# One product for B and C, dt out of the scores, two-bank VectorE instructions, and a third of the decay weighing on GpSimd

## What is computed

```
proj = rmsnorm(modulated layernorm(x)) @ in_proj_w.T      # z 256, x_ssm 256, B 128, C 128, dt 4
xh   = silu(causal conv of x_ssm, 4 taps);  dt = softplus(dt_raw + dt_bias);  dA = exp(-exp(A_log) * dt)
h_t  = h_{t-1} * dA_t + (dt_t * xh_t) B_t;  y_t = h_t . C_t + D * xh_t     # 4 heads of 64
x1   = x + ga * (h_in + (y * silu(z)) @ out_proj_w.T)
logits = rmsnorm(modulated layernorm(x1)) . slots;  dispatch = softmax over tokens, combine = softmax over slots
out  = x1 + gb * combine( experts( dispatch(x) ) )
```

## Time and profile before

| | us |
|---|---|
| median of 3 runs (230.20 to 232.47) | 231.29 |
| span of the profiled execution | 227.2 |
| busy: PE / PEld | 205.5 (90%) / 148.2 (65%) |
| busy: DVE / ACT / POOL | 139.5 (61%) / 120.3 (53%) / 60.9 (27%) |
| chain that ended last, by engine | PE 68%, DVE 11%, ACT 11%, POOL 4%, DMA 3% |
| granted TensorE clock | 1.00 (2.4 GHz) throughout |

### The profile page before, as it was taken

One profiled execution on the slowest core, in us unless ns is written; L12 is line 12 of the kernel. 1 busy time (PEld: TensorE's weight loads), 2 busy tenths in 40 slices (PEclk: granted clock), 3 DMA queues, 4 the chain that ended last, 5 costly groups with the idle time before them and its releaser, 6 DMA issues.

```text
span 227.2 us, 4247 instructions
## 1 busy us (share of the span) xinstructions
PE 205.5 (90%) x1575; PEld 148.2 (65%) x1575; DVE 139.5 (61%) x372; ACT 120.3 (53%) x264; POOL 60.9 (27%) x147
## 2 busy tenths in 40 slices
PE   3879979995799899998978799989999999999995
PEld 2445555673377795475656387765865948659995
DVE  3887868998999956859988875730130221302753
ACT  3879896533468856797531566658327062270000
POOL 6545885016524203984015600000000000000000
PEclk9999999999999999999999999999999999999999
DMA  6404000200600000000500000006222141200122
GB/s 189 118 6 140 1 5 8 87 3 11 197 24 3 0 0 3 1 2 7 183 0 1 0 3 0 0 3 185 49 84 61 42 139 49 85 10 3 46 69 69
DMA packets 15344, 10.72 MB, mean 47 GB/s; under 512 B 1773, under 2 KB 13654, under 8 KB 15326
## 3 DMA queue, kind: packets, MB, share of 16 engines
q1 hardware_dynamic: 15100, 10.31, 15.5%
q10 hardware_dynamic: 226, 0.16, 0.2%
HBM read 9.34 MB, written 1.07 MB: 46 GB/s over the span
## 4 chain that ended last, share of the span: by engine, by line
PE 68%; DVE 11%; ACT 11%; POOL 4%; DMA 3%; issue 2%; ACTq 1%; DVEq 0%; POOLq 0%
PE bank L577 28%; PE bank L922 13%; PE bank L904 11%; PE bank L761 4%; PE bank L814 3%; PE bank L750 2%; POOL root L490 2%; DVE xcT L1309 2%; DVE bst L1183 2%; ACT zsT L1066 2%; PE bank L829 2%; DMA vec_nat<-ffn_slot_norm_gamma_dram 2%; ACT xhT L1072 1%; PE bank L835 1%; PE bank L860 1%
## 5 line engine op out<-in xcount | busy, mean ns | idle before, releaser
L1446 DVE TENSOR_TENSOR eo<-bank,seg_e 128x512 f32<-128x512 f32 x8 | 5.5, 692 | 47.9 <-PE bank L922 47.9
L922 PEld LDWEIGHTS bank<-w_sb,zsT 128*64 128x64 f32 x256 | 27.8, 137 | 3.0 <-issue 3.0
L922 PE MATMUL bank<-w_sb,xcT 128*64 128x128 f32 x256 | 28.8, 273 | 0.0
L922 PE MATMUL bank<-w_sb,zsT 128*64 128x128 f32 x256 | 28.8, 273 | 0.0
L922 PEld LDWEIGHTS bank<-w_sb,xcT 128*64 128x64 f32 x256 | 27.8, 137 | 0.0
L904 PE MATMUL bank<-slotsT,w_sb 128*128 128x512 f32 (+1 forms) x64 | 26.1, 558 | 0.2 <-ACT zsT L1140 0.2
L1140 ACT ACTIVATE zsT<-bank,vecT 128x512 f32<-128x512 f32 x16 | 10.7, 687 | 24.9 <-PE bank L904 24.9
L577 PE MATMUL bank<-xnT,winT 128*128 128x512 f32 x48 | 23.0, 607 | 0.3 <-ACT BT L1053 0.3
L490 POOL TENSOR_TENSOR root<-root,neg_half 128x2 f32<-128x2 f32 (+1 forms) x24 | 20.2, 842 | 2.0
L904 PEld LDWEIGHTS bank<-slotsT,w_sb 128*128 128x128 f32 x64 | 11.4, 190 | 12.6 <-issue 12.1
L1309 DVE SCALAR_TENSOR_TENSOR xcT<-bank,convw,xcT 128x510 f32<-128x510 f32 (+2 forms) x24 | 17.3, 737 | 3.6 <-ACT xcT L1050 3.3
(11 more groups left out here) (165 smaller groups left out, 414.9 us busy)
## 6 DMA issues: line engine op xcount, KB each, us to landing
w_sb<-in_L_ffn_w_dram SPq DMA_DIRECT2D x16, 256.0 KB, 2.9
mods_bc<-mod_dram SPq DMA_DIRECT2D x4, 320.0 KB, 3.5
xin<-in_L_attn_x_dram SPq DMA_DIRECT2D x4, 256.0 KB, 3.1
out_dram<-x1tok SPq DMA_DIRECT2D x16, 64.0 KB, 1.5
mods_bc<-mod_dram SPq DMA_DIRECT2D x4, 192.0 KB, 3.3
seg_e<-mod_dram SPq DMA_DIRECT2D x1, 512.0 KB, 3.8
eo<-in_L_attn_in_proj_w_dram SPq DMA_DIRECT2D x1, 384.0 KB, 4.1
eo<-in_L_wmod_dram SPq DMA_DIRECT2D x1, 256.0 KB, 4.6
```

What stands on the lines that cost most here:

```text
L922: q = nc.tensor.matmul(o[j * S:(j + 1) * S, tile_cols(b)], act_h[j][k // 2][:, k % 2, at:at + S], w2_sb[j][:, k, :], start=k == 0 and b == ...
L1446: V.tensor_tensor(o, bank[4 + 2 * (it % 2) + g][:, :].rearrange("p (b d) -> p b d", d=P), b2_bc[:, it, :].unsqueeze(1).broadcast_to((P, 4, ...
```

## The change

1. B and C are no longer projected. Once, at the start, TensorE multiplies the two 128x128 blocks of the weights; with that product U = (M xn) of one projection, and G = xn_s . U_t, so `scores` takes xnT itself as one operand. U is copied by `copy_u` (with the norm's weight as scale).
2. The four dt columns are appended to U (`dt_columns`, GpSimd, once), so dt_raw comes out of the score matmuls: 260 and 132 columns in place of 256 and 128. `dt_in` reads `gm`, after `copy_scores`. Scores now go to banks 4j+3 and 4j+2, before z, and no longer wait for the convolution.
3. PSUM is one tensor `banks`; `dt_times_x`, `token_max`, `slot_max` and `norm_slots` run once over both halves in place of twice.
4. `weigh(2)` and `weigh(5)` become `weigh_last(0)` and `weigh_last(1)` on GpSimd; `decay(5)` and `y_of` wait for them.
5. All tables of turns are new, SP's too; `rsm_rows(1)` goes from turn 13 to 30, `slots` and `xn2T` have tiles of their own, `mod_rows` shares `combT`.

```diff
 
+            def dt_columns():
+
+                pool.wait_ge(s_act0, ACT_WIN)
+                for j in range(2):
+                    nc.gpsimd.tensor_copy(ut[j][:, :, L:L + H], winT[:, U0 + P:U0 + GB].unsqueeze(1).broadcast_to((P, BP, H))
+                                          ).then_inc(s_ut, 1)
...
+            def weigh_last(bi):
+                def visit(j, it):
+                    wait(pool, g_done, j, it, bi + 1)
+                    wait(pool, seg_done, j, it, 3 * bi + 3)
+                    if bi:
+                        wait(pool, y_ps, j, it, 1)
+                    else:
+                        wait_before(pool, disp_done, j, it)
+                    s = gm[j][:, bi * GW + L + H:(bi + 1) * GW - H]
+                    nc.gpsimd.tensor_tensor(seg_m[j][:, 2, :].rearrange("p (h t) -> p h t", h=H),
+                                            seg_e[j][:, 2, :].rearrange("p (h t) -> p h t", h=H),
+                                            s.unsqueeze(1).broadcast_to((P, H, P)), ALU.mult
+                                            ).then_inc(m_last_done[1][j], 1)
+                return visit
...
                 wait(pe, xnT_done, j, it)
                 if it == 0:
                     pe.wait_ge(s_act0, (ACT_WIN, ACT_SN)[j])
-                for t in range(TP):
-                    q = mm(b3[:, t * H:(t + 1) * H], xnT[j][:, tile_cols(t)], winT[:, DT0:ROWS])
-                q.then_inc(proj_ps[1][j], 1)
+                wait_before(pe, slotsT_done, j, it)
+                mm(b2[:, :], winT[:, U0:U0 + P], xnT[j][:, :]).then_inc(proj_ps[1][j], 1)
 
                 wait_before(pe, slots_done, j, it)
                 mm(b0[:, :], winT[:, X0:X0 + P], xnT[j][:, :]).then_inc(proj_ps[1][j], 1)
                 mm(b1[:, :], winT[:, X0 + P:X0 + 2 * P], xnT[j][:, :]).then_inc(proj_ps[1][j], 1)
-                wait_before(pe, slotsT_done, j, it)
-                mm(b2[:, :], winT[:, B0:B0 + P], xnT[j][:, :]).then_inc(proj_ps[1][j], 1)
+
+            def scores(j, it):
+
+                wait(pe, ut_done, j, it)
+                if it == 0:
+                    pe.wait_ge(s_ut, j + 1)
+                for bi in range(BP):
+                    o = bank[4 * j + 3 - bi]
+                    mm(o[:, 0:L + H], xnT[j][:, tile_cols(bi * NT)], ut[j][:, bi, :])
+                    mm(o[:, L + H:GW], xnT[j][:, tile_cols(bi * NT + 1)], ut[j][:, bi, P:L + H]).then_inc(g_ps[1][j], 1)
 
             def project2(j, it):
 
-                wait(pe, nabs_done, j, it)
-                mm(bank[4 * j + 3][:, :], winT[:, C0:C0 + P], xnT[j][:, :]).then_inc(proj_ps[1][j], 1)
-                wait(pe, xbc_done, j, it, 3)
-                mm(bank[4 * j + 2][:, :], winT[:, Z0:Z0 + P], xnT[j][:, :]).then_inc(z_ps[1][j], 1)
+                wait(pe, g_done, j, it, 1)
+                mm(bank[4 * j + 3][:, :], winT[:, Z0:Z0 + P], xnT[j][:, :]).then_inc(z_ps[1][j], 1)
 
             def project3(j, it):
-                wait(pe, xbc_done, j, it, 4)
-                mm(bank[4 * j + 3][:, :], winT[:, Z0 + P:Z0 + 2 * P], xnT[j][:, :]).then_inc(z_ps[1][j], 1)
-
-            def scores(j, it):
-
-                wait(pe, xbc_done, j, it)
-                for bi in range(BP):
-                    wait(pe, conv_done, j, it, bi + 1)
-                    o = bank[4 * j + bi]
-                    t0 = bi * L
-                    mm(o[:, 0:L], BT[j][:, t0:t0 + P], CTr[j][:, t0:t0 + L])
-                    mm(o[:, L:L + P], BT[j][:, t0 + P:t0 + L], CTr[j][:, t0 + P:t0 + L]).then_inc(g_ps[1][j], 1)
+                wait(pe, g_done, j, it, 2)
+                mm(bank[4 * j + 2][:, :], winT[:, Z0 + P:Z0 + 2 * P], xnT[j][:, :]).then_inc(z_ps[1][j], 1)
...
-                    wait(pe, m_done, j, it, 3 * bi + 3)
+                    wait(pe, m_done, j, it, 2 * bi + 2)
+                    wait(pe, m_last_done, j, it, bi + 1)
...
-            visits = [((2, 7, 61, 64), t_xn), ((4, 9, 65, 68), project1), ((6, 11, 66, 70), project2),
...
+            visits = [((2, 7, 61, 64), t_xn), ((3, 10, 65, 68), project1), ((8, 13, 72, 70), project2),
...
+
+            def copy_u(j, it):
+                wait(act, proj_ps, j, it, 1)
+                A(ut[j][:, :, 0:L], bank[4 * j + 2][:, :].rearrange("p (b t) -> p b t", b=BP), ACT.Identity,
+                  scale=vecT[:, RNW:RNW + 1]).then_inc(ut_done[1][j], 1)
...
             def dt_in(j, it):
-                wait(dve, proj_ps, j, it, 1)
+                if it == 0:
+                    dve.wait_ge(s_small, N_SMALL)
                 d = dv[j]
-                step(j, it, V.tensor_tensor(d[:, VV, :].rearrange("p (t h) -> p t h", h=H),
-                                            bank[4 * j + 3][:, 0:TP * H].rearrange("p (t h) -> p t h", h=H),
-                                            dtb_row[:, :].unsqueeze(1).broadcast_to((P, TP, H)), ALU.add))
+                wait(dve, g_done, j, it)
+                step(j, it, V.tensor_tensor(d[:, VV, :].rearrange("p (b n h) -> p b n h", b=BP, n=NT),
+                                            gm[j][:, 0:BP * GW].rearrange("p (b c) -> p b c", b=BP)[:, :, P:GW]
+                                            .rearrange("p b (n c) -> p b n c", c=GB)[:, :, :, P:GB],
+                                            dtb_row[:, :].unsqueeze(1).unsqueeze(1).broadcast_to((P, BP, NT, H)), ALU.add))
...
             def dt_times_x(j, it):
-                for bi in range(BP):
-                    wait(dve, xht_ps, j, it, bi + 1)
-                    V.tensor_tensor(
-                        dtx[j][:, bi * NT:(bi + 1) * NT, :].rearrange("p t (h d) -> p (t h) d", h=H),
-                        bank[4 * j + bi][:, :].rearrange("p (g d) -> p g d", d=HD),
-                        dv[j][:, DTH, bi * NT * H:(bi + 1) * NT * H].unsqueeze(2).broadcast_to((P, NT * H, HD)),
-                        ALU.mult).then_inc(dtx_done[1][j], 1)
+                wait(dve, xht_ps, j, it)
+                V.tensor_tensor(
+                    dtx[j][:, :, :].rearrange("p t (h d) -> p (t h) d", h=H),
+                    banks[:, 4 * j:4 * j + 2, :].rearrange("p b (g d) -> p (b g) d", d=HD),
+                    dv[j][:, DTH, :].unsqueeze(2).broadcast_to((P, TP * H, HD)), ALU.mult).then_inc(dtx_done[1][j], 1)
...
             def slot_max(bi):
                 def visit(j, it):
-                    for m2 in range(2):
-                        wait(dve, ls_ps, j, it, 2 * bi + m2 + 1)
-                        with nc.allow_low_precision("the shift of a softmax"):
-                            q = V.reduce_max(cshift[j][:, 2 * m2:2 * m2 + 2],
-                                             bank[4 * j + (0, 2)[bi] + m2][:, :].rearrange("p (m t) -> p m t", m=2), AX.X)
-                    q.then_inc(cshift_done[1][j], 1)
+                    n0 = 4 * j + (0, 2)[bi]
+                    wait(dve, ls_ps, j, it, 2 * bi + 2)
+                    with nc.allow_low_precision("the shift of a softmax"):
+                        V.reduce_max(cshift[j][:, :].rearrange("p (n m) -> p n m", n=2),
+                                     banks[:, n0:n0 + 2, :].rearrange("p n (m t) -> p n m t", m=2), AX.X
+                                     ).then_inc(cshift_done[1][j], 1)
                 return visit
```

201 lines of the change are left out of this document (99 added, 102 removed).

## The result

| | before | after |
|---|---|---|
| median, us (4 runs each) | 231.38 (230.20 to 232.47) | 235.35 (233.80 to 236.19) |
| ratio after / before, 95% interval | | 1.016 (1.010 to 1.022) |
| span of the profiled execution | 227.2 | 231.7 |
| busy PE / PEld | 205.5 / 148.2 | 204.1 / 146.6 |
| busy DVE / ACT / POOL | 139.5 / 120.3 / 60.9 | 134.6 / 121.9 / 72.3 |

What follows compares the result with a forecast made beforehand. No single engine was taken as bound around the scans, but a relay among four; 2.1 + 1.3 from the rounds, 0.4 from softmax, 0.5 back, net 3.3, gave span 223.9 and time 228.0 us, range 224.2 to 231.2.

Steps and rivals of the forecast that it cites:

- a gain of 3.3 us: Whole kernel: 2.1 from round 0, 1.3 from round 1, 0.4 from softmax stages, 0.5 back for collisions; net 3.3 us.
- rival (1): TensorE was the bound all along, so its 7.6 us come off whole, giving 223.7 us; chance 0.16.
- Walk of round 0: Scan of round 0: first exp at 33.1 to 33.3, last output projection at 52.9 instead of 55.00; minus 2.1 us.
- Walk of round 1: Scan of round 1: first y products at 107.8 behind GpSimd's queue, last output projection 122.5 instead of 123.81; minus 1.3 us.
- 1.3 and 0.9 a pass: VectorE: 1.3 us a pass from weighings that leave, near 0.9 us a pass from two-bank forms and small reciprocals.
- The merged forms: Two-bank VectorE operations: waits for the second half, 0.4 to 0.6 us each, priced at nothing; 0.4 us gained in softmax stages.
- the list of what would prove me wrong: Signs: first exp at 34.6 or later, GpSimd weighings near 1.9 or VectorE's near 1.2, TensorE waiting for merged reductions.
- The two extra table loads: ScalarE, round 0, in the queue to ksm: two more loads of 1283 ns, 2.6 us; 5.3 by the skill's drain rule.
- Rival (2): Round 0 gives nothing: loads, late dt and rsm1 eat its gains, only round 1's 1.3 us remain; 230.0 us, chance 0.25.
- Rival (3): GpSimd's queue decides each y, its operations held 0.45 us each beside VectorE; 234.3 us at worst, chance 0.13.
- The 4.1 us stay: Whole kernel: the median 231.29 lies 4.1 us over the profiled span 227.2; this was added to the forecast span 223.9.

Runs made afterwards that it cites:

- the filled kernel: The changed kernel plus 15 matmuls that nothing reads, ahead of TensorE's waits (8 in round 0, 7 in round 1): 233.45 us, ratio 1.0047 to the kernel before.
- the control without products: The kernel before with GpSimd's basis and gate products cut to 4 of 128 columns: 231.47 against 231.62 us, ratio 0.9988.

## Why the prediction was wrong

By the ratios, the loss of 3.7 us is 2.6 of clock (1.0 to 4.2) and 1.5 of GpSimd's products (0.3 to 2.7); by the medians 235.35, 233.45 and 231.10 it would be 1.9 and 2.4. With both gone the changed kernel stands 0.4 us under the kernel before (from 1.2 under to 0.4 over), and level with it when that has the same cut (0.9983 and 0.9988). So two things went wrong: two costs that I left out, and a gain of 3.3 us that is not there even without them.

*The clock: the step that failed.* "Half of the removed matmuls stand where TensorE would then wait" was used against rival (1) only. I took TensorE idle time as free, because the trace of before has its clock at 1.00 throughout. That was one execution: in 29 later runs of the kernel before the mean clock was between 0.978 and 1.000, mostly 0.993; in the control without products (0.993) the clock was at 0.50 for 3.4 us behind the scan of round 0, from 56.7. No term of the sum allowed for it. What the runs showed in its place: 13.6 us at 0.50 in two stretches and a mean of 0.971, 2.6 us of the result.

*Walk of round 0: the other step that failed.* Three of the four table loads are where I put them (20.46, 25.55, 27.07), and ksm came at 29.43 as forecast. The fourth, at 31.8 in the walk (33.1 less 1.28), started at 33.34. I had VectorE's convolution of pass 1 from 27.0 to 31.5, "just in time" for the last silus; it ran from 28.14 to 32.66. The cast of 1.02 us and the operation of 0.63 beside GpSimd are 1.3 us more than twice 0.17, and moving the basis group away brought the load, w and the first exp forward by that much. So of the 2.1 to 2.3 us by which the first exp missed its mark (35.36 for 33.1 to 33.3), 1.5 are the load.

The rest, 0.7 us, is TensorE. I went from ksm to the first decay block without the second running sums, which stand between them in its queue and wait for w of pass 1 at 33.38, where it was 30.80 before. At full clock this costs the first exp nothing: in the filled kernel the sums wait for w just so (33.72), and the exp follows its load without a gap:

```profile
33.68 1.28 ACT L1127 ACT_TABLE_LOAD   x1
33.72 0.22 POOL L584 TENSOR_TENSOR dv<-dv,expA_t 128x16 f32<-128x16 f32 x1
...
34.98 1.09 ACT L1127 ACTIVATE seg_e<-banks 128x512 f32<-128x512 f32 x2
```

*Walk of round 1.* Against its late start, ksm of pass 0 at 102.76 is right (102.2 to 102.7), the first y 2.7 us later than forecast (110.05). I had it bound by GpSimd's queue; GpSimd was through at 109.03, about as the walk has it (106.4 and 2.25 of late start), and then idle for 1.91 us until the third decay was there:

```profile
107.62 1.41 POOL L549 TENSOR_TENSOR eo<-woT,mods_bc 128x256 f32<-128x256 f32 x2
110.94 1.28 POOL L535 TENSOR_TENSOR seg_m<-seg_e,gm 128x512 f32<-128x512 f32 x1 [1.91 <-issue]
```

What was late was TensorE: 1.95 and 1.91 us for the two groups of xh transposes against 1.06 at full clock, and the decays behind ksm of pass 1 at 106.36, which waited for the slowed casts.

*Durations.* GpSimd's weighing was right, 1347 ns in the mean for the forecast 1.27 us, with 1.77 at worst:

```profile
L535 POOL TENSOR_TENSOR seg_m<-seg_e,gm 128x512 f32<-128x512 f32 x8 | 10.8, 1347 | 10.2 <-ACT seg_e L1118 7.8 <-issue 2.4
```

VectorE's own rose from 723 ns to 844. Its busy time fell by 4.9 us, where my parts add up to 8.8 (1.3 and 0.9 a pass). The 0.9 was too much by its own terms: five pairs at 0.07 and two small reciprocals of 0.18 make 0.7.

*Costed at nothing.* The merged forms: 1.0 us in the kernel before. TensorE waits 0.56 and 0.57 us for the slot maxima in the changed one, as the list of what would prove me wrong had it.

*Costed and free.* The two extra table loads, 2.6 us, gave nothing when they went. Rival (2) made its case from them and from dt behind the scores: the first exp did come later than 34.6, but not for the loads. No load shows a drain ahead of it here either (ScalarE idle 0.0 before 25.55), so the larger price of the Trainium skill's "ScalarE: Activation LUTs" is not borne out, and on this path neither price mattered.

*Rival (3)*, 0.13 in all and 0.09 for a loss, came nearest: contention of GpSimd and VectorE, up to 234.3, with the first y of round 1 later than 110 (112.75, or 110.5 against the late start). But it had GpSimd held, at its products and weighings, and between softplus and the gate products GpSimd was not: 102.19 to 109.03 is the 6.8 us that the walk gave it. It is VectorE that was held, at its smallest operations, 16 columns wide, where each can wait for a whole 1.3 us operation of GpSimd; in round 0 this reached the path through the convolution behind them, in round 1 through the parts ahead of ksm of pass 1. I had the rule for that (the Trainium skill, "SBUF — State Buffer", SBUF: two separate sides: the other engine waits in full) and applied it to the wide operations only. The trace agrees with it: the cast of 1.02 us ends at 27.82, GpSimd's sum at 27.78, and the operations of 1.18 and 0.65 us at 103.79 and 105.01 stand beside basis groups in the same way.

*The sum against the median.* "The 4.1 us stay" was also wrong in kind: between time and span lie 1.9 to 2.4 us in nearly every later run, 2.9 at most. The rest was that the profiled execution of before was a short one, 227.2 where the median span of its later runs is 229.8; the inputs were early in it (xnT at 12.23, in other executions of such kernels at 14.3).

*What stays open:* where the 3.3 us went that the walks gained on paper. Dt behind the scores takes perhaps 0.7 of it and the merged forms up to 1.0, neither shown in the changed kernel, and the exp of dt of pass 1 in round 0, 3.0 us later than before, was freed in no run that left the rest in order. Nor did I separate in time what GpSimd's products cost by holding VectorE and what by standing in GpSimd's own queue; in round 0 the trace speaks for VectorE, since GpSimd, through with its basis group, stood idle for 1.91 us until the reciprocal was there. And no run filled the gaps of the kernel before, so what its own falls of the clock cost is not known.

## What to carry to other kernels

Work that is removed from an engine which others keep waiting makes its gaps longer, and on TensorE a longer gap can cost twice: look at the granted clock in slices of 2 us around each wait, and price what follows a gap at the slower level. When an engine is given more work beside VectorE, list VectorE's smallest operations on the path: each may wait for one whole instruction of the other. And where a walk says "just in time", look at what can hold the earlier engine: the convolution that should have ended just in time was 1.2 us late, and a table load and the whole scan stood behind it.

## What the hardware showed that I had not expected

- With TensorE busy 0.74 us in one slice of 2.00 us and 0.73 in the next, its clock fell to 0.50 within the second and stood there for 6.8 us, to 38.1; in the kernel before one slice at 0.69, between 1.82 and 1.76, left it at 1.00. Matmuls that nothing reads kept it up and were worth 2.6 us (1.0 to 4.2).
- A cast of 16 columns took VectorE 1.02 us beside GpSimd's sum of 512 columns (1.26 us), and a subtraction of the same size 1.18, against 0.17 alone.
- The first copy of xnT moved between 12.2 and 15.7 us from one execution to the next of nearly the same start; a trace's absolute times compare only from a mark behind the inputs.
